# A KAN layer on one core: beta's addition moved from VectorE to ScalarE, and another periodic order on every engine

## The chip, the cores and the metric

One NeuronCore of one Trainium2 chip runs the whole program. The metric is the time of one execution on the device in microseconds. The kernel before takes 10820.42 us (median of three runs, 10817.57 to 10820.53).

## The reference, cut to what matters

The program is a chain of four residual layers on an image tensor of 8 x 32 x 256 x 256 (float32): two hyperbolic convolutions, a pole-residue operator, a KAN layer on 8 x 8 windows, and a local pattern layer. Only the third, the KAN layer, is changed. Its reference, with `_layernorm` as usual (gain, bias, eps 1e-5):

```python
def _fastkan(x, ln_g, ln_b, ws, wb, bb):
    ln = _layernorm(x, ln_g, ln_b)
    basis = jnp.exp(-((ln[..., None] - GRID) / DENOM) ** 2)     # 8 grid points, -2 to 2
    flat = basis.reshape(*basis.shape[:-2], -1)
    return flat @ ws.T + jax.nn.silu(x) @ wb.T + bb
y = _layernorm(wins, pn_g, pn_b)          # over the 32 channels of a pixel
a = _fastkan(y, grouped by columns of a window, k1)
d = _fastkan(y, grouped by rows of a window, k2)
e = _fastkan(y, over the channels, k3)
z = _fastkan(a + d + e, over the channels, k4)
out = z + wins
```

(The two lines for a and d are in words: the reference reshapes the window, applies the layer to 16 features and reshapes back.)

## The kernel before, in words

`window_layer` (L1658) computes the KAN layer in 64 tiles (32 bands of 8 rows, two halves of the images each). A tile is 128 partitions x 2048 float32. Five normalisations are made per tile: PN (the plain one, whose result plus beta is y) and those of K1 to K4 (the four KANs). Their steps, with the engine that runs each (the function names are those of the code):

- **Transfers, all issued by SyncE (SP), in order.** LOAD_X (`load_x`, L1775): the tile into `x`. FEED_Y K1 and K2 (`feed_y`, L1791): y and its transposed copy, regrouped in 8 DMAs each into `kin`. KEEP_U (`keep_u`, L1799): silu(y) to DRAM, FEED_U (`feed_u`, L1803): back in 8 DMAs into `ku`. BACK K1 (L1812, 16 DMAs) and BACK K2 (L1821, 8 DMAs): the results of K1 and K2 regrouped from `ku` into `back_k1` and `back_k2`. LOAD_R (L1781): the tile again, into `x_to_x`. STORE (L1787): the result out of `x_to_x`.
- **Normalisation.** CENTER (TensorE) into the one PSUM tile `norm`; MOVE (ScalarE) out of it; SQUARE (ScalarE) into the one tile `sq`; VARIANCE (TensorE); LOG and ROOT (ScalarE, 128 x 128); SPREAD (TensorE); SCALE (VectorE, `scale`, L1984). `norm` serves all five kinds in turn, so each of these TensorE steps waits until the step before it in `norm` has been taken out (`norm_banks_free`, L2050). After SCALE PN, BETA (`add_beta`, L1991) adds pn_b to y in place and lets go `normed`, for which TURN_Y (L1959, VectorE: the transposed copy), SILU PN (ScalarE), FEED_Y K1 and CENTER K3 wait.
- **The basis.** Of the 8 basis functions numbers 0 and 4 are made by ScalarE (`anchor`, L1903: a square; `exp`, L1909) and the other six by VectorE (`grow`, L2006), each the one before it times `ratio`. RATIO (`growth`, L1914, ScalarE) fills the one tile `ratio` and so waits until all growths of the kind before are done. The 8 results of a kind pass through `ex`, a ring of 6 buffers: a new one waits until TensorE has used the one 6 places before (`buffer_free`, L1733).
- **The products** (`products`, L2125, TensorE): for each basis function 32 matmuls into the one PSUM tile `out`; ahead of number 4 the other terms (`others`, L2099): silu's product, for K3 also `back_k1`, for K4 also `x_to_x`. EVAC (`evacuate`) takes `out` away: ScalarE for K1, K2, K4 (L1922), VectorE for K3 (L1995, 3.8 us, which adds `back_k2` and gives `z`, the input of K4). MEASURE (L2016, VectorE) takes statistics of the result.

SCALE PN of a tile overwrites the y of two tiles before, so it waits for that tile's anchor 4 and RATIO of K3 (`read_by_bases`, L1724). FEED_Y of a tile waits for the anchors and RATIO of the tile before, and FEED_U K1 for the landing of BACK K1 of the tile before.

**The order is written out by hand.** For each step the tables at L1610 to L1634 hold a position; a period has 256 units. `rounds` (L1766) runs 64 + 6 rounds, and in each an engine runs its steps in the order of position modulo 256; the quotient says how many tiles the step lags behind the round. So position / 256 is no time: the tables fix only the order within an engine, and engines meet in semaphores. `grow 5 K3 (4)` below is growth 5 of K3 for tile r - 4 in round r. Where an engine's list is begun is free; each begins here close to RATIO K3, and an item from the next round is counted from this round's number.

The orders before, one period on each engine:

```
SP: FEED_Y K2 (2); BACK K1 (3); KEEP_U K1 (2); LOAD_R (4); FEED_U K1 (2); LOAD_X (0); BACK K2 (3); STORE (4); FEED_Y
  K1 (1); KEEP_U K2 (2); FEED_U K2 (2)
ACT: RATIO K3 (5); SQUARE K2 (4); ROOT K3 (4); ROOT PN (3); anchor4 K3 (5); LOG K2 (4); EVAC K4 (6); exp4 K3 (5);
  SILU_TURNED (4); anchor0 K1 (4); ROOT K2 (4); exp0 K1 (4); RATIO K1 (4); SILU PN (3); MOVE PN (2); anchor4 K1 (4);
  SQUARE PN (2); SILU K4 (5); LOG PN (2); exp4 K1 (4); MOVE K4 (5); anchor0 K2 (4); SQUARE K4 (5); exp0 K2 (4); LOG K4
  (5); RATIO K2 (4); MOVE K1 (3); ROOT K4 (5); anchor4 K2 (4); EVAC K1 (4); exp4 K2 (4); SQUARE K1 (3); MOVE K3 (3);
  anchor0 K4 (5); SQUARE K3 (3); exp0 K4 (5); RATIO K4 (5); LOG K1 (3); EVAC K2 (4); LOG K3 (3); anchor4 K4 (5); ROOT
  K1 (3); exp4 K4 (5); MOVE K2 (3); anchor0 K3 (4); exp0 K3 (4)
DVE: grow 1,2,3 K3 (4); SCALE PN (2); grow 5,6,7 K3 (4); SCALE K3 (3); BETA (2); grow 1 K1 (3); EVAC K3 (4); SCALE K2
  (3); grow 2,3,5,6,7 K1 (3); TURN_Y (2); grow 1,2 K2 (3); SCALE K4 (4); grow 3,5,6,7 K2 (3); MEASURE (5); grow
  1,2,3,5,6,7 K4 (4); SCALE K1 (2)
PE: SPREAD K1 (3); prod 4,5,6 K4 (5); VARIANCE K2 (3); prod 7 K4 (5); SPREAD PN (2); prod 0,1,2,3 K3 (4); SPREAD K3
  (3); prod 4,5 K3 (4); CENTER PN (1); prod 6,7 K3 (4); SPREAD K2 (3); prod 0 K1 (3); VARIANCE PN (1); prod 1 K1 (3);
  CENTER K4 (4); prod 2,3,4 K1 (3); VARIANCE K4 (4); prod 5 K1 (3); CENTER K1 (2); prod 6,7 K1 (3); SPREAD K4 (4);
  prod 0 K2 (3); CENTER K3 (2); prod 1,2,3 K2 (3); VARIANCE K1 (2); prod 4,5,6,7 K2 (3); VARIANCE K3 (2); prod 0 K4
  (4); CENTER K2 (2); prod 1,2,3 K4 (4)
```

Of the kernel before, what the change touches and what calls it, by code (L numbers as in the profile page):

```python
# [25 lines left out]
ALU = mybir.AluOpType  # L26
ACT = mybir.ActivationFunctionType
# [1507 lines left out]
def prepare_kan(net, k, scale, bias):  # L1535
    nc, ins = net.nc, net.ins
    with ExitStack() as local:
# [26 lines left out]
        def _(dve):  # L1564
# [37 lines left out]
PN, K1, K2, K3, K4 = range(5)  # L1602
# [31 lines left out]
KEEP_U = {K1: 612, K2: 740}  # L1634
# [23 lines left out]
def window_layer(net, k, source, bias, target, stats):  # L1658
# [9 lines left out]
    with ExitStack() as local:  # L1668
# [39 lines left out]
        vec = k["kan_vec"]  # L1708
# [135 lines left out]
        def _(act):  # L1844
            a = nc.scalar
# [38 lines left out]

            def silu_turned(t):
# [41 lines left out]
            def round_(now):  # L1927
                for u in range(UNITS):
# [566 lines left out]
```

## Time and profile before

| what | value |
|---|---|
| median of three runs | 10820.42 us |
| the profiled execution | 10825.04 us, its span 10823.3 us |
| busy over the whole span | PE 8523.8, DVE 8580.3, ACT 7651.5 us |
| steady part of the KAN layer, 5400 to 9800 us | DVE 3827.19, ACT 3783.63, PE 3553.68 us busy of 4400 |

The whole program runs 10823 us; the KAN layer fills the stretch from about 4394 us (its first load) to 10054 us (its last statistics), over half. The last row is the one to read: there neither VectorE nor ScalarE is full, each has about an eighth of the time idle, and the same pattern of waits comes back in every tile. The other layers are not touched.

### The profile page before, as it was taken

Reading aid. Unit: us, or ns where it says so; the run is one execution under the profiler, and the core shown is the slowest. Engines: PE = TensorE matmul, PEld = TensorE weight load, DVE = VectorE, ACT = ScalarE, POOL = GpSimd, SP = SyncE. Lnnn points to the kernel's source line nnn. Section 1 sums busy time; section 2 is a strip of 40 time slices with the busy share of each in tenths; the row PEclk is TensorE's granted clock in tenths of the full one; section 3 lists DMA queues with packets and bytes.
Section 4 is the critical chain, followed back from the end, with each engine's and each line's share of the span. In section 5 each row is a group of like instructions: output and inputs, shape, how many; then the busy total and the mean of one; then the engine's idle time right before and its main releaser. Section 6 shows DMA issues by size and latency. Waiting matters only on the chain. (4 is left out here: it accounts for less than half of the span.)

```text
span 10823.3 us, 360441 instructions
## 1 busy us (share of the span) xinstructions
PE 8523.8 (79%) x162984; PEld 4456.5 (41%) x162984; DVE 8580.3 (79%) x7730; ACT 7651.5 (71%) x5904; POOL 0.2 (0%) x4
## 2 busy tenths in 40 slices
PE   0898879996665799578888788788878888787788
PEld 0344433333442688233433344333334443333445
DVE  6777756666777588588888888888888888888788
ACT  0555545554552555588888888888888888887788
POOL 0000000000000000000000000000000000000000
PEclk9999989998887899699999999999989999999899
DMA  7999879996663588355555555555555555554566
GB/s 291 249 257 259 239 215 265 266 263 209 270 271 121 153 278 277 100 136 132 136 137 138 132 136 136 139 134 135 138 132 137 134 137 136 136 133 115 171 209 195
DMA packets 1210907, 1960.32 MB, mean 181 GB/s; under 512 B 133280, under 2 KB 954400, under 8 KB 1122720
## 3 DMA queue, kind: packets, MB, share of 16 engines
q1 hardware_dynamic: 1209376, 1937.26, 64.7%
q8 instruction: 1284, 21.04, 0.8%
q14 instruction: 247, 2.02, 0.1%
HBM read 852.00 MB, written 545.26 MB: 129 GB/s over the span
## 5 line engine op out<-in xcount | busy, mean ns | idle before, releaser
L2013 DVE SCALAR_TENSOR_TENSOR ex<-ratio,ex 128x2048 f32<-128x2048 f32 x1536 | 3507.4, 2290 | 455.5 <-issue 256.9
L2139 PE MATMUL out<-ex,kan_basis 32*32 32x512 f32 x65536 | 2691.8, 634 | 466.5 <-ACT ku L1925 210.3
L2139 PEld LDWEIGHTS out<-ex,kan_basis 32*32 32x32 f32 x65536 | 1115.4, 105 | 1426.4 <-issue 605.4
L556 PE MATMUL conv<-uc,w 128*32 128x512 f32 x12288 | 1447.9, 597 | 16.4 <-DMA uc<-u 16.2
L463 ACT ACTIVATE v<-conv,cb 128x512 f32<-128x512 f32 x512 | 350.6, 685 | 904.7 <-PE conv L556 414.3
L1912 ACT ACTIVATE ex<-ex 128x2048 f32<-128x2048 f32 x512 | 975.5, 1905 | 2.2
L556 PEld LDWEIGHTS conv<-uc,w 128*32 128x32 f32 x12288 | 489.8, 109 | 727.4 <-issue 673.8
L2272 DVE TENSOR_TENSOR d<-xt 128x2313 f32<-128x2313 f32 (+2 forms) x256 | 621.4, 2495 | 98.8 <-PE acc L2326 98.5
L2326 PE MATMUL acc<-d,weights 32*32 32x512 f32 x16384 | 628.9, 606 | 81.9 <-issue 76.1
L1906 ACT ACTIVATE ex<-y,offset 128x2048 f32<-128x2048 f32 x128 | 256.8, 2006 | 401.3 <-issue 398.7
L2085 PE MATMUL norm<-sq,c_kan_ones 128*32 128x128 f32 x10240 | 399.5, 304 | 172.3 <-ACT sq L1869 109.6
L2294 ACT ACTIVATE d<-d,steep 128x2313 f32<-128x2313 f32 (+2 forms) x256 | 533.7, 2159 | 0.6 <-DVE d L2272 0.6
L2095 PE MATMUL norm<-roots,c_sel 32*128 32x128 f32 x10240 | 392.8, 288 | 159.6 <-ACT x L1862 84.3
L1906 ACT ACTIVATE ex<-kin,offset 128x2048 f32<-128x2048 f32 x256 | 511.1, 1997 | 5.3 <-issue 5.1
L660 DVE TENSOR_TENSOR u<-xn,spread 128x512 f32<-128x512 f32 (+2 forms) x320 | 379.3, 1219 | 170.2 <-PE spread L521 168.0
L2095 PEld LDWEIGHTS norm<-roots,c_sel 32*128 32x128 f32 x10240 | 328.9, 190 | 439.6 <-ACT x L1862 137.9
L2085 PEld LDWEIGHTS norm<-sq,c_kan_ones 128*32 128x32 f32 x10240 | 299.3, 121 | 505.8 <-issue 278.9
L2326 PEld LDWEIGHTS acc<-d,weights 32*32 32x32 f32 x16384 | 330.1, 103 | 327.3 <-issue 217.9
L1850 ACT ACT_TABLE_LOAD x261 | 334.9, 1283 | 180.7 <-PE norm L2085 142.2
L2000 DVE SCALAR_TENSOR_TENSOR z<-out,kan_vec,back_k 128x2048 f32<-128x2048 f32 x64 | 243.1, 3798 | 194.2 <-DMA back_k<-ku 164.8
L513 PE MATMUL pc<-sqv,c_ones 128*32 128x256 f32 x2048 | 314.7, 380 | 91.0 <-ACT sqv L464 91.0
L443 ACT ACTIVATE xn<-xt,bias,scale 128x2560 f32<-128x2560 f32 x128 | 322.6, 2522 | 69.5 <-DVE u L660 63.1
(276 smaller groups left out, 14357.2 us busy)
## 6 DMA issues: line engine op xcount, KB each, us to landing
uc<-u SPq DMA_DIRECT2D x2048, 129.0 KB, 3.6
xt<-in_x SPq DMA_DIRECT2D x128, 1024.0 KB, 7.3
t<-v SPq DMA_DIRECT2D x128, 1024.0 KB, 7.0
ku<-kept_silu SPq DMA_DIRECT2D x1024, 128.0 KB
xt<-in_x SPq DMA_DIRECT2D x32, 2048.0 KB, 7.4
xt<-t SPq DMA_DIRECT2D x64, 1024.0 KB, 6.7
tt<-t SPq DMA_DIRECT2D x64, 1024.0 KB, 12.0
x<-x SPq DMA_DIRECT2D x64, 1024.0 KB, 4.9
```

The lines of the kernel that those rows point to most:

```text
L463: a.activation(v_rows, src, ACT.Identity, bias=cb[:, 0:1])
L556: last = m.matmul(conv[QUAD * b:QUAD * b + QUAD, k % 2, :], w_sb[:, o, d, :], uc[:, h, b, 2 * p:2 * p + 2, d:d + COLS], start=(d == 0), st ...
L660: return v.tensor_tensor(inside(u[:, h, first_row:first_row + rows, 1:COLS + 1]), inside(xn[:, h, at].rearrange("p (r w) -> p r w", w=COLS ...
L1906: a.activation(base_buffer(kind, ANCHORS[j], t), norm_out(kind, t % 2), ACT.Square, bias=k["offset"][:, kind - 1, ANCHORS[j]:ANCHORS[j] + ...
L1912: a.activation(base_buffer(kind, ANCHORS[j], t), base_buffer(kind, ANCHORS[j], t), ACT.Exp, scale=-1.0).then_inc(exps[kind], 1)
L2013: v.scalar_tensor_tensor(base_buffer(kind, n, t), ratio[:], LARGEST, base_buffer(kind, n - 1, t), ALU.min, ALU.mult).then_inc(grown[kind], 1)
L2085: last = m.matmul(norm[rows(quarter), 0, 0:P], k["c_kan_ones"][:, 0 if kind in (K1, K2) else 1, i, :], sq[:, block_:block_ + P], start=(i ...
L2095: last = m.matmul(norm[:, quarter, P * i:P * i + P], k["c_sel4"][rows(quarter), i, :], roots[rows(quarter), kind, :], start=(i == 0), stop ...
L2139: last = m.matmul(out[rows(i), g, :], k["kan_basis"][rows(g), kind - 1, n, :], base[rows(g), cols(i)], start=(n == 0), stop=(n == BASES - ...
L2272: v.tensor_tensor(d[:, h, n, rows, columns], there, xt[:, parity, h, rows, columns], ALU.subtract).then_inc(diff_ready, 1)
L2294: a.activation(t, t, ACT.Tanh, scale=steep[:, h:h + 1]).then_inc(tanh_ready, 1)
L2326: last = m.matmul(acc[quad(k), h, g, :], weights[quad(g), n, :], source_tile[quad(g), row + 2 * k:row + 2 * k + 2, column:column + COLS], ...
```

## The change

`add_beta` is taken from the VectorE block and written for ScalarE, as an ACTIVATE Identity with the same bias vector and the same semaphore. And every position of the tables is new. No buffer, no wait and no transfer is added or removed.

```diff
--- before.py
+++ after.py
@@ -1607,31 +1607,31 @@
 GROWTHS = tuple(n for n in range(BASES) if n not in ANCHORS)
 EXP_SET, SILU_SET = "natural_log_exp_and_others", "silu_and_others"
 UNITS = 256
-CENTER = {PN: 535, K1: 869, K2: 951, K3: 886, K4: 1346}
-MOVE = {PN: 612, K1: 928, K2: 1051, K3: 972, K4: 1409}
-SQUARE = {PN: 617, K1: 966, K2: 1060, K3: 991, K4: 1419}
-VARIANCE = {PN: 576, K1: 925, K2: 962, K3: 947, K4: 1376}
-LOG = {PN: 630, K1: 1012, K2: 1065, K3: 1029, K4: 1423}
-ROOT = {PN: 806, K1: 1046, K2: 1083, K3: 1061, K4: 1445}
-SPREAD = {PN: 714, K1: 955, K2: 1072, K3: 1004, K4: 1392}
-SCALE = {PN: 697, K1: 916, K2: 1022, K3: 982, K4: 1352}
-EVACUATE = {K1: 1196, K2: 1272, K3: 1276, K4: 1578}
-RATIO = {K1: 1088, K2: 1178, K3: 1312, K4: 1515}
-ANCHOR = {K1: (1079, 1127), K2: (1157, 1190), K3: (1310, 1319), K4: (1495, 1547)}
-EXP = {K1: (1084, 1146), K2: (1164, 1216), K3: (1311, 1327), K4: (1511, 1559)}
-GROW = {K1: {1: 1000, 2: 1040, 3: 1042, 5: 1048, 6: 1058, 7: 1059},
-        K2: {1: 1074, 2: 1085, 3: 1098, 5: 1109, 6: 1110, 7: 1112},
-        K3: {1: 1176, 2: 1204, 3: 1205, 5: 1210, 6: 1217, 7: 1220},
-        K4: {1: 1383, 2: 1405, 3: 1407, 5: 1411, 6: 1421, 7: 1424}}
-PRODUCT = {K1: (1081, 1089, 1097, 1104, 1119, 1123, 1126, 1133),
-           K2: (1139, 1149, 1159, 1172, 1182, 1184, 1188, 1192),
-           K3: (1227, 1242, 1258, 1259, 1274, 1288, 1310, 1312),
-           K4: (1462, 1464, 1465, 1466, 1469, 1472, 1473, 1475)}
-SILU = {PN: 836, K4: 1391}
-TURN_Y, SILU_TURNED, BETA, MEASURE = 809, 1073, 727, 1632
-LOAD_X, LOAD_R, STORE = 145, 1133, 1187
-FEED_Y, FEED_U, BACK = {K1: 431, K2: 575}, {K1: 655, K2: 784}, {K1: 866, K2: 914}
-KEEP_U = {K1: 612, K2: 740}
+CENTER = {PN: 630, K1: 954, K2: 1042, K3: 1000, K4: 1455}
+MOVE = {PN: 587, K1: 931, K2: 1024, K3: 979, K4: 1434}
+SQUARE = {PN: 597, K1: 975, K2: 1055, K3: 984, K4: 1438}
+VARIANCE = {PN: 685, K1: 1016, K2: 1112, K3: 1035, K4: 1496}
+LOG = {PN: 651, K1: 991, K2: 1070, K3: 1010, K4: 1453}
+ROOT = {PN: 752, K1: 1009, K2: 1078, K3: 1044, K4: 1463}
+SPREAD = {PN: 828, K1: 1047, K2: 1148, K3: 1119, K4: 1497}
+SCALE = {PN: 652, K1: 896, K2: 981, K3: 936, K4: 1277}
+EVACUATE = {K1: 1216, K2: 1267, K3: 1224, K4: 1578}
+RATIO = {K1: 1083, K2: 1195, K3: 1314, K4: 1518}
+ANCHOR = {K1: (1079, 1087), K2: (1176, 1230), K3: (1306, 1320), K4: (1493, 1531)}
+EXP = {K1: (1082, 1154), K2: (1181, 1233), K3: (1312, 1324), K4: (1506, 1532)}
+GROW = {K1: {1: 955, 2: 957, 3: 982, 5: 991, 6: 992, 7: 1001},
+        K2: {1: 1011, 2: 1018, 3: 1034, 5: 1037, 6: 1042, 7: 1043},
+        K3: {1: 1155, 2: 1162, 3: 1176, 5: 1177, 6: 1182, 7: 1183},
+        K4: {1: 1300, 2: 1324, 3: 1336, 5: 1346, 6: 1384, 7: 1385}}
+PRODUCT = {K1: (1158, 1186, 1198, 1201, 1204, 1226, 1232, 1239),
+           K2: (1244, 1252, 1270, 1271, 1275, 1278, 1284, 1289),
+           K3: (1359, 1361, 1369, 1370, 1376, 1379, 1392, 1396),
+           K4: (1550, 1553, 1556, 1558, 1566, 1571, 1572, 1612)}
+SILU = {PN: 830, K4: 1371}
+TURN_Y, SILU_TURNED, BETA, MEASURE = 733, 1062, 825, 1517
+LOAD_X, LOAD_R, STORE = 242, 1191, 1317
+FEED_Y, FEED_U, BACK = {K1: 533, K2: 653}, {K1: 734, K2: 835}, {K1: 957, K2: 1011}
+KEEP_U = {K1: 585, K2: 735}
 MOVED_BY_ACT = (PN, K1, K2, K3, K4)
 SQUARED_BY_ACT = (PN, K1, K2, K3, K4)
 EVACUATED_BY_ACT = (K1, K2, K4)
@@ -1882,6 +1882,10 @@
                     tables(SILU_SET)
                     a.activation(W[:], Z[:], ACT.Silu).then_inc(u_ready[kind], 1)
 
+            def add_beta(t):
+                act.wait_ge(scaled[PN], t + 1)
+                a.activation(Y[:, t % 2], Y[:, t % 2], ACT.Identity, bias=vec[:, 1:2]).then_inc(normed, 1)
+
             def silu_turned(t):
                 act.wait_ge(copied_y, t + 1)
                 act.wait_ge(kin_loaded[K2], 128 * t + 128)
@@ -1931,6 +1935,8 @@
                             silu(kind, t)
                     if (t := now.due(u, SILU_TURNED)) is not None:
                         silu_turned(t)
+                    if (t := now.due(u, BETA)) is not None:
+                        add_beta(t)
                     for kind in NORMS:
                         if kind in MOVED_BY_ACT and (t := now.due(u, MOVE[kind])) is not None:
                             move(kind, t)
@@ -1988,10 +1994,6 @@
                 v.scalar_tensor_tensor(norm_out(kind, t % 2), norm_in(kind, t % 2), ln_g[kind], norm_flat,
                                        ALU.mult, ALU.mult).then_inc(scaled[kind], 1)
 
-            def add_beta(t):
-                dve.wait_ge(scaled[PN], t + 1)
-                v.tensor_scalar(Y[:, t % 2], Y[:, t % 2], vec[:, 1:2], None, ALU.add).then_inc(normed, 1)
-
             def evacuate(kind, t):
                 dve.wait_ge(used, serial(kind, BASES, t))
                 if kind == K3:
@@ -2038,7 +2040,7 @@
                         for n in GROWTHS:
                             if (t := now.due(u, GROW[kind][n])) is not None:
                                 grow(kind, n, t)
-                    for position, step in ((TURN_Y, turn_y), (BETA, add_beta), (MEASURE, measure)):
+                    for position, step in ((TURN_Y, turn_y), (MEASURE, measure)):
                         if (t := now.due(u, position)) is not None:
                             step(t)
             rounds(round_)
```

The orders after, one period on each engine, in the notation from above:

```
SP: FEED_Y K1 (2); STORE (5); FEED_U K2 (3); KEEP_U K1 (2); FEED_Y K2 (2); LOAD_R (4); BACK K1 (3); FEED_U K1 (2);
  KEEP_U K2 (2); LOAD_X (0); BACK K2 (3)
ACT: RATIO K3 (5); SILU_TURNED (4); anchor4 K3 (5); EVAC K4 (6); exp4 K3 (5); LOG K2 (4); ROOT K2 (4); anchor0 K1 (4);
  BETA (3); exp0 K1 (4); RATIO K1 (4); SILU PN (3); anchor4 K1 (4); MOVE PN (2); SQUARE PN (2); SILU K4 (5); exp4 K1
  (4); LOG PN (2); anchor0 K2 (4); MOVE K4 (5); exp0 K2 (4); SQUARE K4 (5); MOVE K1 (3); RATIO K2 (4); LOG K4 (5);
  ROOT K4 (5); EVAC K1 (4); anchor4 K2 (4); SQUARE K1 (3); exp4 K2 (4); MOVE K3 (3); anchor0 K4 (5); SQUARE K3 (3);
  LOG K1 (3); exp0 K4 (5); RATIO K4 (5); ROOT PN (2); ROOT K1 (3); LOG K3 (3); EVAC K2 (4); anchor4 K4 (5); exp4 K4
  (5); MOVE K2 (3); ROOT K3 (3); anchor0 K3 (4); SQUARE K2 (3); exp0 K3 (4)
DVE: SCALE K1 (3); grow 1,2 K3 (4); SCALE PN (2); grow 3,5,6,7 K3 (4); SCALE K3 (3); grow 1,2 K1 (3); EVAC K3 (4);
  SCALE K2 (3); grow 3 K1 (3); TURN_Y (2); grow 5,6,7 K1 (3); MEASURE (5); grow 1,2 K2 (3); SCALE K4 (4); grow 3,5,6,7
  K2 (3); grow 1,2,3,5,6,7 K4 (4)
PE: prod 4,5,6 K4 (6); SPREAD PN (3); prod 7 K4 (6); prod 0,1 K3 (5); VARIANCE K2 (4); prod 2,3 K3 (5); SPREAD K3 (4);
  prod 4,5,6,7 K3 (5); CENTER PN (2); SPREAD K2 (4); prod 0,1 K1 (4); VARIANCE PN (2); prod 2 K1 (4); CENTER K4 (5);
  prod 3,4 K1 (4); CENTER K1 (3); prod 5,6,7 K1 (4); VARIANCE K4 (5); SPREAD K4 (5); prod 0,1 K2 (4); CENTER K3 (3);
  prod 2,3 K2 (4); VARIANCE K1 (3); prod 4,5,6,7 K2 (4); VARIANCE K3 (3); prod 0,1 K4 (5); CENTER K2 (3); prod 2,3 K4
  (5); SPREAD K1 (3)
```

## Rows read from the trace of the kernel before

**Rows 1.** Busy time in the steady stretch of the KAN layer (busy per engine, clock, DMA share).

```profile
core 0: us, PE busy (x) PEld busy (x) DVE busy (x) ACT busy (x) POOL busy (x), PEclk, DMA share, GB/s
5400.00:9800.00 4400.00, 3553.68 (x83580) 1746.88 (x83592) 3827.19 (x1876) 3783.63 (x2535) 0.00 (x0) 0.91 0.56 135
```

**Rows 2.** VectorE's EVAC K3, once per tile: min/median/max ns, first and last start.

```profile
L2000 DVE SCALAR_TENSOR_TENSOR z<-out,kan_vec,back_k x64: 3680/3808/3828, 4552.0 to 10005.9; 128x2048 f32<-128x2048 f32 x64
```

**Rows 3.** VectorE in order of time: start, duration, [idle before, releaser].

```profile
7021.36 13.80 DVE L2013 SCALAR_TENSOR_TENSOR ex<-ratio,ex 128x2048 f32<-128x2048 f32 x6 [1.15 <-ACT ratio L1920]
...
7043.17 4.62 DVE L2013 SCALAR_TENSOR_TENSOR ex<-ratio,ex 128x2048 f32<-128x2048 f32 x2 [3.55 <-issue]
7048.94 2.35 DVE L1988 SCALAR_TENSOR_TENSOR y<-x,kan_vec,norm 128x2048 f32<-128x2048 f32 x1 [1.15 <-PE norm L2095]
...
7065.83 3.81 DVE L2000 SCALAR_TENSOR_TENSOR z<-out,kan_vec,back_k 128x2048 f32<-128x2048 f32 x1 [1.83 <-DMA back_k<-ku]
...
7077.40 6.95 DVE L2013 SCALAR_TENSOR_TENSOR ex<-ratio,ex 128x2048 f32<-128x2048 f32 x3 [0.97 <-ACT ex L1912]
...
7086.75 4.62 DVE L2013 SCALAR_TENSOR_TENSOR ex<-ratio,ex 128x2048 f32<-128x2048 f32 x2 [0.38 <-ACT ratio L1920]
```

**Rows 4.** TensorE in the same period: the other terms and products of K4.

```profile
7034.90 2.22 PE L2115 MATMUL out<-x_to_x,grown 32*32 32x512 f32 x32 [4.28 <-DMA x_to_x<-x]
7037.05 4.80 PE L2123 MATMUL out<-silu_z,kan_silu 128*128 128x512 f32 x8
7041.78 3.41 PE L2139 MATMUL out<-ex,kan_basis 32*32 32x512 f32 x96
```

**Rows 5.** SP's queue in order of time: start, time to issue, DMAs.

```profile
7005.50 5.86 SPq L1796 DMA_DIRECT2D kin<-columns_first  x8
7011.46 12.33 SPq L1818 DMA_DIRECT2D back_k<-ku  x16
...
7024.51 2.92 SPq L1785 DMA_DIRECT2D x_to_x<-x  x4
7029.19 9.00 SPq L1810 DMA_DIRECT2D ku<-kept_silu  x8
7051.31 2.31 SPq L1779 DMA_DIRECT2D x<-x  x4
7053.72 6.21 SPq L1824 DMA_DIRECT2D back_k<-ku  x8
...
7068.83 6.32 SPq L1796 DMA_DIRECT2D kin<-y  x8
```

**Rows 6.** ScalarE in the same period: start, duration, [idle before, releaser].

```profile
7003.44 2.00 ACT L1906 ACTIVATE ex<-kin,offset 128x2048 f32<-128x2048 f32 x1
7005.33 1.97 ACT L1925 ACTIVATE ku<-out,kan_vec 128x2048 f32<-128x2048 f32 x1
...
7045.27 2.01 ACT L1906 ACTIVATE ex<-y,offset 128x2048 f32<-128x2048 f32 x1 [5.83 <-issue]
```

**Rows 7.** Groups, 6400 to 8400 us: mean ns of one; ScalarE, VectorE.

```profile
L1912 ACT ACTIVATE ex<-ex 128x2048 f32<-128x2048 f32 x184 | 350.6, 1905 | 0.7
...
L1850 ACT ACT_TABLE_LOAD x92 | 118.0, 1283 | 54.7 <-PE norm L2085 50.4 <-DVE y L1993 2.3
...
L1906 ACT ACTIVATE ex<-y,offset 128x2048 f32<-128x2048 f32 x46 | 92.3, 2007 | 144.4 <-issue 144.4
...
L1993 DVE TENSOR_SCALAR y<-y,kan_vec 128x2048 f32<-128x2048 f32 x23 | 29.4, 1280 | 0.0
```

**Rows 8.** Groups, 6400 to 8400 us: TensorE's silu products of K4 and K3.

```profile
L2123 PE MATMUL out<-silu_z,kan_silu 128*128 128x512 f32 x184 | 116.3, 789 | 0.0
...
L2123 PE MATMUL out<-silu_y,kan_silu 128*128 128x512 f32 x184 | 85.1, 605 | 0.0
```

**Rows 9.** Busy time in 2 us of the same period (columns as in rows 1).

```profile
7036.00:7038.00 2.00, 2.00 (x26) 0.50 (x2) 2.00 (x2) 2.00 (x2) 0.00 (x0) 0.50 0.31 97
```

**Rows 10.** DMA issues by line over the span: count, KB each, us to landing.

```profile
uc<-u SPq DMA_DIRECT2D x2048, 129.0 KB, 3.6
```

## The prediction, made before the kernel was run

> **What bounds the kernel now.** I read the busy time first, by stage. In the steady stretch of the KAN layer VectorE is busy 3827 of 4400 us, ScalarE 3784, TensorE 3554 [rows 1]: 87, 86 and 81%. None is full. The period comes from VectorE's EVAC K3, once per tile: (10005.9 - 4552.0) / 63 = 86.57 us [rows 2]. Per tile that is 75.3 us of VectorE's work and 11.3 idle, and 74.4 us of ScalarE's and 12.1 idle. So a loop of waits through several engines sets the period, and the next view is the one in order of time.
>
> One period of VectorE shows six gaps [rows 3]: 3.55 us before growth 2 of K3 (put down to "issue": it waits for a buffer of the ring), 1.15 before SCALE PN, 1.83 before EVAC K3 (back_k2 has not landed), 0.97 before growth 5 of K1, 0.38 and 1.15 before growths that wait for RATIO. TensorE says what the 3.55 are: it stood 4.28 us for `x_to_x`, then needed 2.22 + 4.80 us for K4's other terms before product 4 [rows 4], and that product frees the buffer. ScalarE stood 5.83 us for its own buffer at the same time [rows 6]. SP's queue says why `x_to_x` is late [rows 5]: anchor 4 of K2 ends at 7005.44 [rows 6], FEED_Y K2 starts at 7005.50 (so a hand-off is about 0.1), takes 5.86 to issue, BACK K1 behind it 12.33, and only then LOAD_R starts, at 7024.51. The loop is anchor 4 of K2, FEED_Y K2, BACK K1, LOAD_R, product 4 of K4, the ring, and through ScalarE to anchor 4 of the next K2. The transfers' order, not an engine, is the bound.
>
> **The beta step.** VectorE loses 1.28 us per tile [rows 7]. ScalarE gains an ACTIVATE that no row shows (Identity, SBUF to SBUF, with a bias vector). Nearest are its squares with a bias vector, 2.01 us, and at the other end exp without one, 1.905 [rows 7]; an instruction overlaps its successor by 0.1 (2.00 long, the next one 1.89 later [rows 6]). I take 1.9 added, bounds 1.8 and 2.0. It stands between anchor 0 and exp 0 of K1 and uses no table of its own, so the four table loads per tile (92 in 23 tiles [rows 7]) stay four: the new list still changes set four times. Work per tile becomes 74.0 on VectorE and 76.3 on ScalarE. The row says that this addition costs VectorE 1.28 and a ScalarE square of that size 2.01. A rule speaks against the move: the Trainium skill, page "ScalarE: Activation LUTs", section "Rules for kernel authors", gives add to the other side: "Use VectorE, not ScalarE". Taken alone it makes this part of the change a loss; it is the slower rival below.
>
> **The transfers' new order.** LOAD_R now follows FEED_Y K2 directly, ahead of BACK K1; STORE stands behind FEED_Y K1, FEED_U K2 behind STORE; LOAD_X and BACK K2 stay in that order, but behind KEEP_U K2. I walk one period, 0 being the end of K4's last growth on VectorE; hand-offs 0.1, growth 2.29, SCALE 2.35, ScalarE's steps as long as their rows less the overlap.
>
> First stretch. RATIO K3 0.1 to 2.1, table load and SILU_TURNED to 5.2. TensorE is in K4's other terms to 2.4 and has product 4 at 3.5, product 6 at 5.7. Anchor 4 of K3 needs product 6: 5.8 to 7.8. Product 7 stands behind SPREAD PN and ends at 8.0; EVAC K4 8.1 to 10.1; table load; exp 4 ends at 13.3. VectorE meanwhile: SCALE K1 (covers RATIO), growths 1 and 2 to 6.9, SCALE PN must wait for anchor 4 (7.9 to 10.3), growth 3, then 0.8 idle until exp 4 is there; the last growth of K3 ends at 20.3.
>
> Second. RATIO K1 follows at 20.4 behind BETA (16.6 to 18.5), which therefore costs nothing here. SCALE K3 covers RATIO; two growths; EVAC K3 from 27.1 (product 7 of K3 ends at 26.0) to 30.8; SCALE K2, growth 3, TURN_Y, three growths to 44.3. ScalarE from RATIO K1 to RATIO K2 has 13 long steps and two table loads, 24.9 us: RATIO K2 at 45.3, one later than VectorE would let it. Growth 1 of K2 at 47.4, 0.4 lost after MEASURE.
>
> Third. K2's growths with SCALE K4 end at 63.3. ScalarE waits 1.5 in MOVE K3: CENTER K3 may not start before SCALE K4 has emptied `norm` (54.3) and takes 2.0. So RATIO K4 runs from 64.1 to 66.1. Nothing stands between K2's last and K4's first growth: 2.9 idle. Six growths end at 79.9. That is the new period: some 5 us of VectorE's gaps instead of 11.3.
>
> Are the transfers covered? LOAD_R: anchor 4 of K2 ends at 51.5, FEED_Y K2 5.9, and 10.4 from LOAD_R's start to its use (7024.51 to 7034.90 [rows 4, 5]): 67.9, wanted at 75.4. BACK K2: from the end of SCALE PN to VectorE's start of EVAC K3 it took 14.5 with the same LOAD_X ahead (7051.29 to 7065.83 [rows 3, 5]): 10.3 + 14.5 = 24.8, wanted at 27.1. FEED_Y K1: anchor 4 of K1 ends at 27.4, 6.3 to issue, a transfer of this size 3.6 to land [rows 10]: 37.4, wanted at 40.4. BACK K1 is issued by 72.4 and wanted a fifth of a period into the next round. FEED_U K1 waits for BACK K1's landing, and KEEP_U K2 behind it for SILU_TURNED; both are through by 8, before LOAD_X may start at 10.3. So each costs nothing, with 7.5, 2.3 and 3.0 us to spare for the three that matter; if one cover is gone, that wait comes in full once per tile.
>
> **Sum.** I take 80.3: the walk's 79.9 and 0.4 for hand-offs over 0.1, of which it has a dozen. Below that, TensorE's clock may give something back. While K4's terms ran after the wait for `x_to_x`, the granted clock was 0.50, 1.2 GHz of 2.4 [rows 9]; a matmul of K4's silu product costs 789 ns on average, one of K3's of the same shape 605 [rows 8]. Without the wait, K4's terms take nearer 4.7 than 7.0 us, EVAC K4 comes earlier, and the walk gives 78.2. The fill (158 us to the first EVAC K3) and drain I leave as they are. 63 x (86.57 - 80.3) = 395 us. Against the profiled execution 10825.0 - 395 = 10430; the median of the runs stands 4.6 lower: 10425.
>
> **Rivals.**
> *A cover is too thin.* One transfer or ScalarE is late by 2 to 5 us per tile, at 83.5 in the middle: 10820 - 63 x 3.1 = 10627. For it: 2.3 us of slack behind a landing that varies, and ScalarE's chain on the path. Against: the measured transfer times are already in the sum. 0.25.
> *ScalarE keeps its idle time.* The place is ScalarE's in-order list, where each wait now holds up 1.9 us more work. If the new order only exchanges its waits for others, the period is 74.4 + 1.9 + 12.1 = 88.4 and the time 10820 + 63 x 1.8 = 10935. It decides from 10.3 us of idle per tile; the walk finds 3 to 4. By the skill's rule on additions, named above, this is where the change should end. 0.07.
> *It does nothing:* the loop through SP is replaced by one equally long, 86.3 to 86.9 per tile: 10820. For it speaks only that the ring, `norm` and `out` stay single. 0.04.
> The forecast (78 to 82 per tile) has 0.64.
>
> **Numbers.** About 0.2% is what a measurement of this kernel can tell from no change: 22 us, or 0.34 us per tile. Faster is forecast and first rival, 0.89; same 0.04; slower 0.07. The range runs from 78.3 per tile (10300) to 83.7 (10640): the walk with K4's terms at the full clock at one end, the middle of the first rival at the other. VectorE's 74.0 plus RATIO K4's uncovered 2.2 is a floor near 10170.
>
> **What would show it.** EVAC K3 once per 80 us. No wait of TensorE for `x_to_x`, none of VectorE for `back_k2`. On VectorE the largest gap between K2's last and K4's first growth, 2.3 to 2.9, released by RATIO; a second one before growth 5 of K3, released by exp. ScalarE about 95% busy, Identity on y near 2 us. SP's LOAD_R straight behind FEED_Y K2. Wrong would be: a gap marked DMA on `kin`, `back_k` or `x_to_x`; a ScalarE idle share still above a tenth; or a period under 78.

## The result, and the profile after

The changed kernel runs in 10647.33 us (median, 10632.8 to 10672.53), the kernel before in 10818.99 us beside it: a ratio of 0.9844, 95% interval 0.9825 to 0.9864. That is 172 us less, where 395 were forecast, and 7 us above the end of the forecast range, 10640. The profiled execution of after took 10672.53 us, its slowest, with a span of 10670.8 us; against before's profiled span it gained 152.5 us.

Where these come from is read first off EVAC K3, as in [rows 2]: tile `z` on VectorE in the kernel after (min/median/max ns, first and last start, and what ended the idle time before it).

```profile
L2002 DVE SCALAR_TENSOR_TENSOR z<-out,kan_vec,back_k x64: 3673/3794/3825, 4556.8 to 9868.2; 128x2048 f32<-128x2048 f32 x64
its engine sat idle before it (us, times) until:
  PE out L2141: 28.0, 31
  PE norm L2097: 11.0, 1
  DMA back_k<-ku: 3.1, 2
```

The period is (9868.2 - 4556.8) / 63 = 84.31 us, before 86.57; predicted was 80.3. 63 x 2.26 = 142 us come from it. The first EVAC K3 starts 4.8 us later than before, and the tail behind the last one is 14.8 us shorter, which closes the account (142.4 - 4.8 + 14.8 = 152.4). So the whole difference to the forecast is in the period. The last line says that the transfer of `back_k2` is covered.

Busy times in the steady stretch of after, with the columns of [rows 1], cut 200 us earlier because the layer ends sooner:

```profile
5400.00:9600.00 4200.00, 3500.76 (x82325) 1699.01 (x82298) 3708.08 (x1799) 3840.02 (x2548) 0.00 (x0) 0.92 0.58 140
```

ScalarE is busy 91%, VectorE 88, TensorE 83. Per tile of 84.31 us VectorE is idle 9.9 us, where the walk had about 5, and ScalarE 7.2. No engine has become the bound.

VectorE of after in order of time, one period (as [rows 3]; the period's end is the end of K4's last growth, 7066.1):

```profile
7069.53 4.62 DVE L2015 SCALAR_TENSOR_TENSOR ex<-ratio,ex 128x2048 f32<-128x2048 f32 x2 [1.15 <-ACT ratio L1924]
...
7079.78 6.95 DVE L2015 SCALAR_TENSOR_TENSOR ex<-ratio,ex 128x2048 f32<-128x2048 f32 x3 [0.58 <-issue]
...
7095.25 3.81 DVE L2002 SCALAR_TENSOR_TENSOR z<-out,kan_vec,back_k 128x2048 f32<-128x2048 f32 x1 [0.82 <-PE out L2141]
7101.23 2.35 DVE L1994 SCALAR_TENSOR_TENSOR kin<-kin,kan_vec,norm 128x2048 f32<-128x2048 f32 x1 [2.17 <-PE norm L2097]
...
7135.56 13.80 DVE L2015 SCALAR_TENSOR_TENSOR ex<-ratio,ex 128x2048 f32<-128x2048 f32 x6 [2.13 <-ACT ratio L1924]
```

The 3.55 us for a buffer of the ring are gone. The gap before K4's growths (2.13) and the one before growth 5 of K3 (0.58) are those that the walk had. New against the walk are gaps of 0.82 us before EVAC K3 and 2.17 us before SCALE K2, which both wait for TensorE. Most of this tile's delay arises on ScalarE in the same stretch:

```profile
7083.10 1.99 ACT L1887 ACTIVATE y<-y,kan_vec 128x2048 f32<-128x2048 f32 x1
...
7092.07 1.28 ACT L1850 ACT_TABLE_LOAD   x1 [3.24 <-PE out L2141]
```

SILU PN's table load (the row at 7092.07) stood 3.24 us for a product of TensorE. The waits of after say the same, from 6400 to 8400 us, which is about 24 tiles (engine, line and releaser: us in total, times, longest):

```profile
DVE ex L2015 <- ACT ratio L1924: 123.4, 77, 3.1
...
PE out L2141 <- ACT x_to_x L1929: 75.5, 24, 3.4
...
ACT logs L1899 <- PE norm L2087: 67.2, 46, 2.9
...
ACT L1850 <- PE out L2141: 35.3, 24, 6.0
```

Three of the four name TensorE. It stands 3.1 us in each tile for EVAC K4 (its result is the tile `x_to_x`), in front of the first product of K3; then LOG K2 stands for VARIANCE K2, and SILU PN for a product. What TensorE does behind its own 3.1 us is in its rows. Two tiles of after:

```profile
7076.52 2.35 PE L2141 MATMUL out<-ex,kan_basis 32*32 32x512 f32 x64 [3.06 <-ACT x_to_x L1929]
7078.80 1.08 PE L2087 MATMUL norm<-sq,c_kan_ones 128*32 128x128 f32 x32
...
7158.48 4.09 PE L2141 MATMUL out<-ex,kan_basis 32*32 32x512 f32 x64 [3.37 <-ACT x_to_x L1929]
7162.49 1.76 PE L2087 MATMUL norm<-sq,c_kan_ones 128*32 128x128 f32 x32
```

The same 64 matmuls take 2.35 us in one tile and 4.09 in the next, and VARIANCE K2 1.08 and 1.76. The granted clock of these stretches is the reason. In the first, the period shown above, it was full, and TensorE's lateness had another source: a pause of 1.82 us inside a group of matmuls, which the last section shows. In the second it is half. Columns as in [rows 1], and PEclk, the granted clock, is the third figure from the end:

```profile
7075.00:7081.00 6.00, 4.48 (x136) 2.21 (x143) 5.42 (x3) 5.34 (x5) 0.00 (x0) 1.00 0.71 194
7158.00:7164.00 6.00, 5.52 (x96) 2.43 (x96) 5.42 (x3) 3.62 (x3) 0.00 (x0) 0.50 0.72 184
7672.00:7678.00 6.00, 4.62 (x76) 1.60 (x80) 5.42 (x3) 4.53 (x3) 0.00 (x0) 0.54 0.71 199
```

At 1.00 it is 2.4 GHz, at 0.50 1.2 GHz. In eight consecutive tiles, from 7066 on, this figure is 1.00, 0.50, 1.00, 0.72, 0.72, 0.72, 0.72 and 0.54. Over the steady stretch, 40 of 49 tiles have some time at the lower clock between 10 and 16 us behind the period's start.

What has improved is K4's own terms, as the prediction had hoped. Groups of after, 6400 to 8400 us, beside [rows 8]:

```profile
L2125 PE MATMUL out<-silu_y,kan_silu 128*128 128x512 f32 x192 | 90.8, 615 | 0.9 <-issue 0.9
L2125 PE MATMUL out<-silu_z,kan_silu 128*128 128x512 f32 x184 | 85.1, 605 | 0.0
```

K4's silu product (`silu_z`) now costs 605 ns where it was 789. The lower clock has left K4's terms, and now falls on the first products of K3, a few us later.

SP's queue, some 30 us earlier, shows that the transfers stand as the change writes them, LOAD_R straight behind FEED_Y K2 and ahead of BACK K1:

```profile
7038.22 6.41 SPq L1796 DMA_DIRECT2D kin<-columns_first  x8
7044.73 2.19 SPq L1785 DMA_DIRECT2D x_to_x<-x  x4
7047.02 12.13 SPq L1818 DMA_DIRECT2D back_k<-ku  x16
```

In all waits of that stretch no engine waits for LOAD_R, which took 4.28 us of TensorE in [rows 4].

### The profile page after: what moved, and what is told of

It reads as the page before. It is cut to its first block and busy times, and to the rows that moved or that the text cites. A ratio compares the mean times of both kernels' runs of the same rounds, so it can differ in the third digit from the quotient of the medians.

```text
span 10670.8 us, 360441 instructions
## 1 busy us (share of the span) xinstructions
PE 8553.0 (80%) x162984; PEld 4435.0 (42%) x162984; DVE 8502.2 (80%) x7666; ACT 7800.9 (73%) x5968; POOL 0.2 (0%) x4
## 5 line engine op out<-in xcount | busy, mean ns | idle before, releaser
L2141 PE MATMUL out<-ex,kan_basis 32*32 32x512 f32 x65536 | 2824.0, 665 | 431.6 <-ACT x_to_x L1929 197.9
L2097 PE MATMUL norm<-roots,c_sel 32*128 32x128 f32 x10240 | 432.2, 310 | 290.7 <-ACT x L1862 171.2
L2097 PEld LDWEIGHTS norm<-roots,c_sel 32*128 32x128 f32 x10240 | 364.2, 209 | 528.2 <-ACT x L1862 228.0
L1994 DVE SCALAR_TENSOR_TENSOR kin<-kin,kan_vec,norm 128x2048 f32<-128x2048 f32 x128 | 300.1, 2344 | 130.6 <-PE norm L2097 130.6
L681 DVE TENSOR_TENSOR v<-v,spread 128x2048 f32<-128x2048 f32 x128 | 292.4, 2285 | 95.3 <-PE spread L521 92.8
```

What stands on the lines that cost most here:

```text
L2097: last = m.matmul(norm[:, quarter, P * i:P * i + P], k["c_sel4"][rows(quarter), i, :], roots[rows(quarter), kind, :], start=(i == 0), stop ...
L2141: last = m.matmul(out[rows(i), g, :], k["kan_basis"][rows(g), kind - 1, n, :], base[rows(g), cols(i)], start=(n == 0), stop=(n == BASES - ...
```

## The experiments

**The two halves.** e1 has the old order with beta on ScalarE, at the new kernel's place (BETA 825); e2 has the new order with beta on VectorE. e0 is the changed kernel once more, run beside e5, e6 and e7. Every ratio is to the kernel before, run beside it. e2's edit, on the changed kernel; e1's is the same function moved the other way, on the kernel before:

```diff
-TURN_Y, SILU_TURNED, BETA, MEASURE = 733, 1062, 825, 1517
+TURN_Y, SILU_TURNED, BETA, MEASURE = 733, 1062, 682, 1517
...
-                a.activation(Y[:, t % 2], Y[:, t % 2], ACT.Identity, bias=vec[:, 1:2]).then_inc(normed, 1)
...
+                v.tensor_scalar(Y[:, t % 2], Y[:, t % 2], vec[:, 1:2], None, ALU.add).then_inc(normed, 1)
```

> The old order of all steps, with only the addition of beta moved to ScalarE (between anchor 0 and exp 0 of K1). Transfer theory: the old period is set by the loop through SP's queue (LOAD_R behind BACK K1, and BACK K2's landing), so VectorE's 1.28 us less per tile are absorbed by its waits and ScalarE's 1.9 us more fall into its 12 us of idle time: between 10800 and 10880 us, no wait of the old kernel gone. Rival (the addition's move is what made the changed kernel faster): at least half of the gain of 172 us, 10735 us or less.

> The new order, with the addition of beta back on VectorE (after SCALE K3, where VectorE waits 1.35 us per tile for RATIO K1). TensorE theory (the new period hangs on TensorE's late products of K3, at the lower clock after its idle gaps): ScalarE's 1.9 us less per tile hardly count, 10600 to 10680 us. ScalarE theory (its list, 77 us of work per tile of 84, is the new bound): 1.5 us or more off each tile, 10555 us or less.

> The changed kernel once more, unaltered, as the yardstick for the three runs beside it: ratio to the kernel before 0.9825 to 0.9864, as in its first comparison.

Measured: e1 10834.85 us, ratio to the kernel before 1.0032 (1.0019 to 1.0045); e2 10664.83 us, 0.9876 (0.9861 to 0.9891); e0 10678.88 us, 0.9847 (0.9831 to 0.9863). Beta's move alone is a small loss. All three lie in the ranges expected. The order alone brings 1.24%, and beta on top of it perhaps 0.3: the intervals of e2 and e0 just touch.

**The order of SP's queue.** e3 is the kernel before with one transfer moved: BACK K1 behind LOAD_R, so that K4's `x_to_x` comes early. e11 takes all eleven of SP's new positions into the kernel before.

```diff
-FEED_Y, FEED_U, BACK = {K1: 431, K2: 575}, {K1: 655, K2: 784}, {K1: 866, K2: 914}
+FEED_Y, FEED_U, BACK = {K1: 431, K2: 575}, {K1: 655, K2: 784}, {K1: 880, K2: 914}
```

> The kernel before with one number changed: BACK K1 comes after LOAD_R on SP's queue instead of ahead of it. Transfer theory: LOAD_R starts some 4 us earlier (then it waits for MEASURE), TensorE's wait for x_to_x and VectorE's 3.5 to 4.1 us gap before growth 2 of K3 go for the most part, 2 to 4 us off each tile: 10565 to 10695 us. Rival (x_to_x's lateness hides another wait of the same length): 10800 to 10830 us.

> The kernel before with SP's eleven positions of the new order and nothing else. Transfer theory: SP's order alone was the bound, so a good part of the gain of 1.5% comes with it, ratio 0.985 to 0.993. Rival (an SP order fits only the compute order it was made with, as in e3_load_r_first, where the wait moved from x_to_x to LOAD_X and BACK K2): ratio 0.995 or more.

Measured: e3 10763.28 us, 0.9957 (0.9943 to 0.9971); e11 10811.28 us, 0.9982 (0.9973 to 0.9991), periods 85.71 and 86.37. The loop of waits that the prediction named as the bound is broken in e3: VectorE's gap before growth 2 of K3 falls from a mean of 4.11 us to 0.03. But the gap before EVAC K3 grows from 3.09 to 7.40. VectorE of e3 in order of time, and its waits:

```profile
7021.75 6.94 DVE L2013 SCALAR_TENSOR_TENSOR ex<-ratio,ex 128x2048 f32<-128x2048 f32 x3
...
7053.81 3.75 DVE L2000 SCALAR_TENSOR_TENSOR z<-out,kan_vec,back_k 128x2048 f32<-128x2048 f32 x1 [10.35 <-PE out L2139]
```

```profile
DVE z L2000 <- PE out L2139: 97.8, 11, 10.8
...
PE norm L2072 <- DMA x<-x: 89.8, 19, 7.9
```

Growths 1 to 3 of K3 now run without a break; but LOAD_X and BACK K2 keep their places behind the rest of SP's queue, so CENTER PN waits 4.7 us for `x`, with products of K3 queued behind it, and EVAC K3 waits for those or for `back_k2`. In e11 it is `back_k2`: 178.3 us in 21 waits. e3's time lies between the two ranges expected, e11's ratio in its rival's. So of the 6 us per tile that the prediction forecast, and the 2.3 that came, moving the transfers alone brings 0.2 to 0.9. The rest of the 2.3 needs the other engines' new orders.

**Is ScalarE the bound?** e5 shortens the new ACTIVATE to one of the tile's 2048 columns. The other columns go on without beta.

```diff
-                a.activation(Y[:, t % 2], Y[:, t % 2], ACT.Identity, bias=vec[:, 1:2]).then_inc(normed, 1)
+                a.activation(Y[:, t % 2, 0:1], Y[:, t % 2, 0:1], ACT.Identity, bias=vec[:, 1:2]).then_inc(normed, 1)
```

> The changed kernel with ScalarE's addition of beta cut to the first of 2048 columns (the other columns stay without beta; no wait changes): ScalarE loses 1.7 us of work per tile. TensorE theory: RATIO K1 comes up to 1.7 us earlier, but SILU PN behind it waits for product 4 of K3 all the same; at most 0.5 us off a tile, 10615 us or more. ScalarE theory: its list is the bound and the whole 1.7 us come off, 10540 us or less.

Measured: 10664.19 us, 0.9832 (0.9812 to 0.9852), period 84.08. The intervals of e5 and e0 overlap by more than half. With some 1.7 us of work less per tile (3761.24 us busy from 5400 to 9600 instead of 3827.65 in e0) ScalarE gives nothing that can be told from zero, as the TensorE theory expected. It simply waits longer: its waits for the product ahead of SILU PN rise from 43.5 us in e0 to 75.4.

**Is it TensorE's work?** e4 leaves out TensorE's silu product of K3 (eight instructions in the trace), so K3's result lacks its silu term.

```diff
-                    else:
+                    elif kind == K4:
```

> The changed kernel without TensorE's silu product of K3 (8 matmuls, 3.7 us per tile), which leaves that term out of the result; no wait and no step of another engine changes. TensorE theory: the products of K3 are on the path that sets the period, so 2 to 3.7 us per tile go, 10410 to 10520 us, and ScalarE's wait before the table load of SILU PN disappears. ScalarE theory: TensorE's lateness costs nothing, 10620 to 10660 us.

Measured: 10570.98 us, 0.9779 (0.9755 to 0.9804), period 82.77. Taking 3.7 us from an engine that is busy 83% brings 1.5 us per tile. Taking 1.7 from the one that is busy 91% brought nothing. TensorE is on the path behind EVAC K4, though the busy shares rank it last. But the time lies between the two ranges expected, above the 10410 to 10520 us of the TensorE theory. Part of the 3.7 us came back, as "issue" in front of its matmuls. Waits of e4, 6400 to 8400 us:

```profile
PE out L2141 <- issue: 50.1, 27, 3.9
```

In after this line is 5.9 us in 8 waits. "Issue" means that the trace shows nothing that the engine waited for. Such stalls of TensorE, nearly all inside a group of matmuls, leave it idle for 2.3 us per tile in e4 between 16 and 28 us behind the period's start, and for 0.65 in after. I didn't find what they wait for.

**Is it TensorE's clock?** Two kernels shorten TensorE's idle time at EVAC K4 in different ways. e6 puts EVAC K4 ahead of anchor 4 of K3 on ScalarE, and lets TensorE reach it: SPREAD PN behind product 7 of K4, VARIANCE K2 behind one more step, SCALE PN one growth later.

```diff
-VARIANCE = {PN: 685, K1: 1016, K2: 1112, K3: 1035, K4: 1496}
+VARIANCE = {PN: 685, K1: 1016, K2: 1115, K3: 1035, K4: 1496}
...
-SPREAD = {PN: 828, K1: 1047, K2: 1148, K3: 1119, K4: 1497}
-SCALE = {PN: 652, K1: 896, K2: 981, K3: 936, K4: 1277}
-EVACUATE = {K1: 1216, K2: 1267, K3: 1224, K4: 1578}
+SPREAD = {PN: 845, K1: 1047, K2: 1148, K3: 1119, K4: 1497}
+SCALE = {PN: 665, K1: 896, K2: 981, K3: 936, K4: 1277}
+EVACUATE = {K1: 1216, K2: 1267, K3: 1224, K4: 1575}
```

e7 leaves ScalarE's order as it is. It moves SPREAD PN behind product 7 of K4 too, and runs SPREAD PN's 16 matmuls (32 instructions in the trace) three times over, which writes the same values again: more work for TensorE, in the place of its idle time.

```diff
-SPREAD = {PN: 828, K1: 1047, K2: 1148, K3: 1119, K4: 1497}
+SPREAD = {PN: 845, K1: 1047, K2: 1148, K3: 1119, K4: 1497}
...
-                for i in range(GROUP):
+                for i in (range(GROUP) if kind != PN else [i for _ in range(3) for i in range(GROUP)]):
```

> The changed kernel with four positions moved, no work and no wait altered: ScalarE's EVAC K4 goes ahead of anchor 4 of K3, TensorE's product 7 of K4 ahead of SPREAD PN and VARIANCE K2 behind product 3 of K3, VectorE's SCALE PN behind growth 3 of K3. TensorE gets `out` back about 2 us earlier and has one short idle stretch there instead of 3.1 us. TensorE theory: LOG K2, product 4 of K3 and EVAC K3 come 1.5 to 3 us earlier and the lower clock in that stretch goes, 2 to 3.5 us off each tile: 10430 to 10530 us. ScalarE theory: ScalarE's work is the same, so 10630 to 10665 us.

> The changed kernel with SPREAD PN behind product 7 of K4 and run three times over (the same values each time), which fills TensorE's 3.1 us of idle time there with 2.1 us of matmuls; SCALE PN comes up to 0.8 us later, which VectorE's wait for exp 4 covers in part. Clock theory: the granted clock stays at its full level in the stretch 8 to 15 us after K4's last growth, and the tile is 1 to 2 us shorter although more work is done, 10520 to 10590 us. Rival (the idle time costs only itself, its filling nothing): the lower clock stays, 10640 to 10700 us.

Measured: e6 10534.09 us, 0.9708 (0.9686 to 0.973); e7 10534.16 us, 0.9713 (0.9697 to 0.9729). Both are some 145 us faster than e0 beside them, though e7 does more work than the changed kernel and takes none away. e7 lies in the clock theory's range, e6 4 us above that of the TensorE theory. TensorE's wait for EVAC K4 in e7 (in total and in one tile), and the clock just behind it in another tile:

```profile
PE out L2141 <- ACT x_to_x L1929: 35.4, 25, 1.6
```

```profile
7080.34 2.96 PE L2097 MATMUL norm<-roots,c_sel 32*128 32x128 f32 x96
7084.60 2.35 PE L2141 MATMUL out<-ex,kan_basis 32*32 32x512 f32 x64 [1.30 <-ACT x_to_x L1929]
7086.88 1.08 PE L2087 MATMUL norm<-sq,c_kan_ones 128*32 128x128 f32 x32
```

```profile
7503.00:7509.00 6.00, 4.70 (x146) 2.24 (x142) 5.56 (x3) 5.39 (x5) 0.00 (x0) 1.00 0.47 147
```

The wait is 1.4 us per tile instead of 3.1. Between 10 and 16 us behind the period's start none of e7's 51 tiles has time at the lower clock, and one of e6's 52, where after has 40 of 49. The steps, as means over 49 or 50 tiles from 5400 to 9600 us, in us from the end of K4's last growth:

```
                      walk   after    e7     e6
EVAC K4 starts         8.1    8.07   7.89   6.16
exp 4 of K3 starts    11.4   11.33  11.15  11.32
LOG K2 starts         13.6   15.16  13.38  13.76
RATIO K1 starts       20.4   21.96  20.24  20.36
load for SILU PN      22.4   25.57  23.14  22.39
EVAC K3 starts        27.1   29.32  27.61  28.05
SCALE K2 starts       30.8   34.38  32.64  31.96
RATIO K2 starts       45.3   49.22  47.37  47.30
RATIO K4 starts       64.1   67.60  65.63  65.52
period                79.9   84.16  82.01  81.81
```

(The prediction doesn't state the walk's values for LOG K2 and SILU PN's load. They follow from EVAC K4's end at 10.1 plus 3.4 us at the full clock, and from RATIO K1's end.)

At EVAC K4 and exp 4 the kernel after is where the walk had it, to 0.1 us; behind them it falls back. In e7 EVAC K4 starts only 0.18 us earlier than in after, and so does exp 4; but LOG K2, for which TensorE still has to do products 0 and 1 of K3 and VARIANCE K2, starts 1.78 earlier, and SILU PN's table load 2.43. In between lies TensorE's work at the one clock or the other: from the start of product 0 to the end of VARIANCE K2 it takes 3.36 us in every tile of e7, and 3.36 to 5.95, on average 4.97, in after. In e6 part of the gain is the earlier EVAC K4 itself: product 0 starts 1.9 us earlier than in after. e7 has the moved SPREAD PN besides the repeats; neither was run without the other. Together they start product 0 only 0.2 us earlier, so 1.6 of the 1.8 us at LOG K2 are the clock's. That it is the repeats, and not the move, that keep the clock up is not shown.

**The same again, and two more gaps filled.** e8 is e6 unaltered. e9 has TensorE, on e6, repeat SPREAD K4 once, and behind VARIANCE K3 work through 28 matmuls on constants (56 instructions in the trace) into a bank of `norm` that is free then. e10 is e6 with beta back on VectorE.

```diff
+                if kind == K3:
+                    for _ in range(7):
+                        for quarter in range(CHUNKS):
+                            m.matmul(norm[rows(quarter), 1, 0:P], k["c_kan_ones"][:, 1, 0, :], k["kan_silu"][:, 0, :],
+                                     start=True, stop=True, tile_position=(0, QUAD * quarter))
...
-                for i in range(GROUP):
+                for i in (range(GROUP) if kind != K4 else [i for _ in range(2) for i in range(GROUP)]):
```

> The kernel of e6_evac_k4_first once more, unaltered, as the yardstick for the two runs that change it: ratio to the kernel before 0.969 to 0.973.

> e6_evac_k4_first with two more of TensorE's idle stretches filled: SPREAD K4 is run twice over (the same values), and behind VARIANCE K3, where TensorE waits for EVAC K2, come 28 matmuls on constants into unused PSUM of the tile norm. Clock theory: the time at the lower clock falls from 10.9 us per tile to 7 or less, and at the 0.26 to 0.38 us per us that the periods of one trace show, 1 to 1.5 us come off each tile: 60 to 95 us less than e6. Rival (these stretches have no path through them, since only the K3 stretch counted): within 20 us of e6, or slower by the 3 us of added matmuls' delay, up to 100 us more.

> e6_evac_k4_first with the addition of beta back on VectorE (behind SCALE K3). With TensorE's lateness gone, VectorE runs from growth 5 of K3 to growth 2 of K1 without a gap, so its 1.28 us should now count: 0.6 to 1.3 us per tile, 40 to 80 us more than e6, although ScalarE has 1.9 us less to do. ScalarE theory: faster than e6.

Measured: e8 10518.6 us, 0.971 (0.9697 to 0.9723); e9 10492.38 us, 0.9682 (0.9669 to 0.9695); e10 10559.06 us, 0.9747 (0.9733 to 0.976). e9 is e8 with nothing but added work on TensorE, and is 26 us faster; its interval lies below e8's. That has the sign of the clock theory, but less than half of the 60 to 95 us that it expected: the time at the lower clock fell from 10.7 us per tile in e8 to 7.8, and the added work takes TensorE's time too. Which of the two fills brought it is not shown. Busy times of e9 in the steady stretch:

```profile
5400.00:9600.00 4200.00, 3602.72 (x89585) 1903.89 (x89576) 3833.42 (x1857) 3970.79 (x2629) 0.00 (x0) 0.95 0.60 145
```

TensorE's clock is 0.95 here, 0.92 in after; ScalarE is now busy 94.5%. e10 against e8 gives what beta's move is worth where ScalarE and VectorE wait less: 40 us in its favour, at the lower end of the 40 to 80 expected, and the intervals lie apart. e9 beats the kernel before by 3.2% and the changed kernel by some 1.6%.

## Why the prediction was wrong in size

It forecast the right sign and the right mechanism for the transfers, and more than twice the gain. The step that failed is in the second stretch of its walk: TensorE's products of K3 were priced at the full clock right behind an idle time of TensorE, and ScalarE's wait for them was left out. That the range's end, 10640, came within 7 us of the result is luck. It was set by a rival in which a transfer or ScalarE is late, and neither was.

**The beta step: right.** Identity on `y` takes 1988 ns, predicted 1.9 net and some 2.0 long; the table loads stay at four per tile (95 in some 24 tiles, 36.6 us of idle before them where it was 54.7 [rows 7]):

```profile
L1887 ACT ACTIVATE y<-y,kan_vec 128x2048 f32<-128x2048 f32 x24 | 47.7, 1988 | 0.0
L1850 ACT ACT_TABLE_LOAD x95 | 121.9, 1283 | 36.6 <-PE out L2141 35.3
```

The rule of the Trainium skill that was weighed against the move ("ScalarE: Activation LUTs", "Rules for kernel authors") is borne out where beta moves alone, by 0.32% (e1), and not in e6's order, where the move gains 40 us of 10559 (e10 and e8). An addition is cheaper on VectorE, 1.28 against 1.99 us, but the queue it stands in decides.

**What bounds the kernel before: half right.** The loop through FEED_Y K2, BACK K1 and LOAD_R was there, and e3 took it away. It was not the only one: a second loop through LOAD_X, BACK K2 and EVAC K3 lay right behind it and took back all but 0.9 us per tile. The walk was of the new orders on all engines and didn't depend on this, but the sentence "the transfers' order, not an engine, is the bound" claimed more than one swap could show.

**The first stretch of the walk: right at its end.** EVAC K4 starts at 8.07 (predicted 8.1), exp 4 at 11.33 (11.4), and K3's last growth ends at 20.27 (20.3), all from the table's means. On the way there RATIO K3 starts at 1.05, not 0.1, since ScalarE is a little behind, and EVAC K4 follows anchor 4 of K3 at once, where the walk had it wait for product 7; the two errors fall on time that was free.

**The second stretch: the step that failed.** "EVAC K3 from 27.1 (product 7 of K3 ends at 26.0)": the walk took TensorE's steps of K3 at the full clock. From product 0's start to product 4's end e7, at the full clock, needs 12.53 us in its median tile, and three more products 3.4; with EVAC K4's end at 10.1 that is the 26.0.

After 3.1 us idle for EVAC K4, TensorE runs many of them at 1.2 GHz: product 0 and 1 in 4.09 us instead of 2.35, VARIANCE K2 in 1.76 instead of 1.08. Between 5 and 30 us from the period's start the trace of after has 4.5 us at the lower clock per tile, e7 0.47, e6 0.66. Against the walk, after is 1.6 us late at LOG K2, 3.2 at SILU PN's table load and 3.6 at SCALE K2; the period is 4.3 us longer. e7 and e6, without the slow clock in that stretch, get 2.2 and 2.4 of these 4.3 back: about half of the miss, most of it already at RATIO K1.

The table places the rest. From RATIO K1 to RATIO K2 the walk had 24.9 us; after takes 27.3, e7 27.1 and e6 26.9. ScalarE's waits there, of which the walk had none, are 2.0, 1.8 and 1.5 us, and its own steps are some 0.4 longer. From RATIO K2 to RATIO K4 all three are 0.4 to 0.6 faster than the walk. Behind RATIO K4 they need 0.5 to 0.8 more, mostly because growth 5 of K4 waits for exp 4 in a third to a half of the tiles (0.7 us per tile in after, 0.4 in e6).

Over 53 periods of after, the one with more time at the lower clock is the longer (correlation 0.64, 0.38 us per us); at none of it the fitted line gives 79.3 us, near the walk's 79.9. TensorE's stalls, 1.2 us per tile over the whole period, go with the period more closely still (correlation 0.78): the 19 periods without one last 82.7 us, the others 84.9, at the same 13.3 us of lower clock. So they are the likely second part of the miss, and the walk had nothing for them. A fit shows no cause by itself. For the clock e7 and e9 do, where more work on TensorE makes the kernel faster; e7 has as much stall time as after. For the stalls no run does.

The prediction had the clock in its sum, and on one side only: as something that K4's terms might give back. They did (789 to 605 ns). It didn't ask where TensorE would stand next, though its own walk had TensorE waiting for the end of EVAC K4 at 10.1. The page "TensorE: Matmul & The Clock Gate" of the Trainium skill, section "A second HAM failure mode: psum-queue depth-cycling", tells of a bf16 kernel in which TensorE idles briefly between groups of matmuls so often that the clock swings between its two levels; the tiles at 1.00, 0.50 and 0.72 side by side agree with that.

**A wait that was missed.** The walk lets SILU PN start behind RATIO K1, at 22.4. It also needs its buffer of `silu_y` back, which K3's silu term of an earlier tile still reads (the trace names product 4 of K3 as the releaser), and for that it stood 1.65 us on average and up to 6.5. The full clock alone doesn't remove this wait. In e7, with 0.47 us of lower clock in the stretch, it is still 0.9 us on average and up to 7.1 (waits of e7, 6400 to 8400 us, some 24 tiles, so 1.0 here):

```profile
ACT L1850 <- PE out L2141: 24.6, 24, 7.1
```

At the full clock and without a stall product 4 ends at 10.1 + 12.53 = 22.6 in the walk's terms, 0.2 behind the 22.4; the longer waits come with stalls and with a later start of product 0. Only in e6, where TensorE starts product 0 at 8.2, is it gone: the table load starts at 22.39.

**Hand-offs: small, as forecast.** 0.4 us were added for them. K3's last growth ends where the walk had it, and six growths without a wait take 13.80 us, which is the walk's 66.1 to 79.9. So the miss isn't in the growths' spacing.

**The transfers: right.** LOAD_R, BACK K2 and FEED_Y K1 are covered. The only wait for one on VectorE is 3.1 us in the whole layer. BACK K2's cover was thin, though. In e6 SCALE PN comes one growth later and LOAD_X, which overwrites what it reads, with it; VectorE then waits for `back_k2` in nearly every tile, some 1 us each (tile `z` on VectorE in e6, as in the first view of after):

```profile
  DMA back_k<-ku: 59.5, 59
```

That is why e6's EVAC K3 starts at 28.05, behind e7's 27.61, though its TensorE is earlier.

**Rivals.** "A cover is too thin", 2 to 5 us late per tile at 83.5 and 10627, had the right size with the wrong engine: it named a transfer or ScalarE. e5 speaks against ScalarE's work, and after's waits against the transfers. "ScalarE keeps its idle time" (88.4 per tile) was wrong, idle there is 7.2 of 84.3 us; e1 is nearest to it, 86.74. "It does nothing" was wrong by 2.3 us per tile. The signs that the prediction gave for being wrong, a gap marked DMA, a ScalarE idle above a tenth or a period under 78, didn't include the one that came: TensorE at the lower clock behind an idle time which the walk itself contained.

**What stays open:** what TensorE's stalls inside its groups in e4 wait for; whether they cost what the fit says; how e6's gain is shared between EVAC K4's earlier start and the clock; and what e9's 81.1 per tile would be without the 7.8 us at the lower clock that are left and the wait for `back_k2`, which it has as e6 does.

## What to carry to other kernels

When a walk over a trace leaves TensorE idle for some us, price its next steps at the lower clock as well, even if it isn't the busiest engine: here that was about half of the difference between 80 and 84 us per tile. Such idle time can be filled with matmuls that write the same values again, or shortened by evacuating `out` first. And list every wait of a step, buffers too: a wait that is nearly covered in the usual tile still costs in the tiles that run late. And when a loop of waits is to be broken, look for the next one as long; in a queue that works in order, moving one transfer forward moves others back.

## What was not expected of the hardware

More matmuls made the kernel faster twice. In e7 SPREAD PN's work is tripled, and with its move behind product 7 of K4 the kernel takes 0.9713 of the time before where the unfilled one takes 0.9847; in e9 28 matmuls on constants and one repeated SPREAD bring 26 us more, and TensorE's granted clock in the steady stretch goes from 0.92 (after) through 0.93 (e6, below) to 0.95.

```profile
5400.00:9600.00 4200.00, 3514.20 (x84561) 1784.08 (x84536) 3810.67 (x1848) 3950.59 (x2616) 0.00 (x0) 0.93 0.59 143
```

The gap of 1.4 to 3.1 us per tile had looked free, since TensorE was the least busy of the three engines. The periods of one execution of the changed kernel, which all do the same work, range from 79.4 to 89.3 us. And a group of 32 matmuls that waits for nothing in the program can stop midway; this one of after stood 1.82 us, with the clock full, and stalls like it took back part of what e4 had freed:

```profile
7086.09 1.09 PE L2110 MATMUL out<-back_k,c_ident 32*32 32x512 f32 x17 [1.82 <-issue]
```
